# Half of a bias addition on VectorE, statistics in SBUF, and two tables made one stage later

## The chip, the cores and the metric

One core of a Trainium2 chip runs the whole program in one launch. The metric is device time in microseconds (us) of one execution; lower is better. The engines are TensorE (PE in the profile), VectorE (DVE), ScalarE (ACT), GpSimd (POOL) and SyncE (SP), whose queue issues most of the transfers.

## The reference

A graph network with four residual layers over 100,000 nodes of 128 features and 50,000 edges, sorted by their receiver. Each layer ends in a layer norm. The change touches the first one:

```python
h = x @ W                                   # 4 heads of 32 columns
alpha = leaky_relu(s_src[row] + s_dst[col])
...
alpha_n = ex / denom[row]
out = segment_sum(alpha_n * h[col], col) + bias
x = layernorm(x + out)
```

Since the weight of a message depends on its receiver's own row `h[col]`, the sum over the edges of one receiver is that row times a sum of weights for each head. So for a node that receives edges the kernel needs, per head, one total, and the layer becomes `layernorm(x + bias + totals * (x @ W))`.

## The kernel before

The program runs nine stages one after the other (`prepare`, `scores_and_sort`, `gat_softmax`, `gat_sums`, `first_layer`, `attention`, `gcn_first`, `gcn_second`, `final_edges`). Each stage ends in `end_stage`, a barrier of all engines. Within a stage every engine runs its own list of instructions, and the engines are ordered by semaphores alone: `then_inc` raises one when an instruction is done, `wait_ge` holds the engine's queue until it is reached.

`gat_sums` sums the attention weights over the edges of each receiver and leaves the totals, turned, in the table `K["totB"]` (128 x 6 x 392: four heads, the degree, and a position). VectorE and ScalarE copy it out of PSUM (L1304, L1337). Then ScalarE takes the root of the degree (L1339), and VectorE makes, in a chain of twenty instructions over 128 x 392 elements (L1308 to L1328), two index tables for later gathers (`idx_a`, `idx_b`) and five tables made from the degree (`dinvB`, `dlastB`, `dinv2B`, `dlast2B`, `degepsB`). In such a chain each instruction waits for the one before it (`link`).

`first_layer` handles the edges in 49 items of 1024 rows, 8 rows on each of 128 partitions. Tiles come in four buffers `u` (`x`, `y`, `o`, the norm's small tiles) or in two (`xT`, `hp`); `tp` has one. For each item:

- SyncE loads `x` (L1456). The load of an item waits until the add (below) of the item four before it is done. SyncE also stores the result `o` (L1460); in its queue the store of an item comes behind the load of the item six later.
- TensorE turns `x` into `tp` (L1483), ScalarE copies that to `xT` (L1499), TensorE multiplies by the weights into `hp` (L1490).
- GpSimd adds the bias to `x` in place (`shift`, L1469), once `x` is turned.
- VectorE multiplies `hp` by the totals of the heads into `y` (`scale`, L1508).
- GpSimd adds `x` to `y` (`add`, L1474).
- VectorE measures mean and variance (`norm_measure`, L1382 to L1399), ScalarE takes the root (L1408), VectorE forms `rs` and `nb` (`norm_scale`, L1419 and L1425), ScalarE applies them in eight instructions (`norm_apply`, L1433).

The order on each engine is written out by hand: `pipeline(engine, (part, lag, count), ...)` runs, in slot s, each part for item s - lag, in the order given:

```python
pipeline(sp, (load, 0, EIGHTS), (store, 6, EIGHTS))
pipeline(pool, (add, 3, EIGHTS), (shift, 1, EIGHTS))
pipeline(pe, (multiply, 1, EIGHTS), (turn, 0, EIGHTS))
pipeline(dve, (measure, 4, EIGHTS), (scale, 2, EIGHTS), (norm_scale, 4, EIGHTS))
```

(ScalarE: copy with lag 0, root with 4, apply with 5; the part names are shortened for `norm_scale`.)

Where the statistics lie is a choice of `norm_of`. Without `ps` all its small tiles are in SBUF. With `ps`, as `first_layer` calls it, the raw statistics, `gap`, `sums` and `squares` lie in one PSUM tile `small`; the odd half of the statistics is first copied to SBUF (L1388), and a second subtraction writes `gap` (L1391) beside `diff` (L1392).

Of the kernel before, what the change touches and what calls it, by code (L numbers as in the profile page):

```python
# [15 lines left out]
ALU = mybir.AluOpType  # L16
ACT = mybir.ActivationFunctionType
F32 = mybir.dt.float32
I32 = mybir.dt.int32

P = 128
N = 100000
E = 50000
D = 128
HEADS = 4
HC = D // HEADS
CHUNKS = 392
EP = CHUNKS * P
SORTN = 65536
SORTF = SORTN // P  # L30
G = 8
# [5 lines left out]
EIGHTS = CHUNKS // 8  # L37
# [1202 lines left out]
def gat_sums(nc, A, T, K):  # L1240
    with ExitStack() as ctx:
# [4 lines left out]
        quarter = CHUNKS // 4  # L1246
        rows = sb("rows", [P, HEADS + 2, 4 * P])
        roots = sb("roots", [P, CHUNKS])
        fallback, known, place = sb("fallback", [P, CHUNKS]), sb("known", [P, CHUNKS]), sb("place", [P, CHUNKS])
        where, bits = sb("where", [P, CHUNKS], I32), sb("bits", [P, CHUNKS], I32)  # L1250
        shift = sb("shift", [P, CHUNKS])
        turned = [ps(f"turned{i}", [P, 4, P]) for i in range(2)]
        turner = turner_of(sb, ps, sem)
        loaded, chain_v, raw_zero = sem("loaded"), sem("chain_v"), sem("raw_zero")
        totals_ready, totals_stored, rows_loaded = sem("totals_ready"), sem("totals_stored"), sem("rows_loaded")
        rows_turned, rows_taken, roots_ready, line_ready, line_stored = sem("rows_turned"), sem("rows_taken"), sem("roots_ready"), sem("line_ready"), sem("line_stored")
        rows_zero, taken_by_act = sem("rows_zero"), sem("taken_by_act")
        warm = sb("warm", [P, 1])
        block = ctx.enter_context(nc.Block())
# [30 lines left out]
        @block.vector  # L1290
        def _(dve):
            link = chain_of(dve, chain_v)
            dve.memset(raw[96:P, E % CHUNKS:, :], 0.0).then_inc(raw_zero, 1)
            link(dve.memset(turner["scr"][:], 0.0))
            link(dve.memset(v[:, HEADS, :], 1.0))
            dve.wait_ge(loaded, 64)
            link(dve.tensor_copy(v[:, 0:HEADS, :], raw[:, :, 0:HEADS].rearrange("p f h -> p h f")))
            link(dve.tensor_copy(v[:, HEADS + 1, :], raw[:, :, HEADS]))
            segment_scan(dve, link, turner, K["seg"], "sum", run[:], v[:, 0:HEADS + 1, :])
            segment_scan(dve, link, turner, K["seg"], "rise", v[:, 0:HEADS + 1, :], run[:])  # L1300
            dve.sem_inc(totals_ready, 1)
            for h in range(0, HEADS + 2, 2):
                dve.wait_ge(rows_turned, h + 1)
                dve.tensor_copy(K["totB"][:, h, :].rearrange("p (r b) -> p b r", b=4), turned[0][:, :, 0:quarter]).then_inc(rows_taken, 1)  # L1304
            dve.wait_ge(taken_by_act, HEADS // 2 + 1)
            dve.wait_ge(rows_taken, HEADS // 2 + 1)
            pos = K["totB"][:, HEADS + 1, :]
            link(dve.tensor_scalar(fallback[:], K["src_idx"][:, 0:CHUNKS], float(EP), None, ALU.add))  # L1308
            link(dve.tensor_scalar(known[:], pos, 0.0, None, ALU.is_ge))
            link(dve.tensor_copy(where[:], pos))  # L1310
            link(dve.tensor_scalar(bits[:], where[:], P - 1, None, ALU.bitwise_and))
            link(dve.tensor_scalar(where[:], where[:], 3 * P, None, ALU.bitwise_and))
            link(dve.tensor_copy(place[:], bits[:]))
            link(dve.tensor_copy(shift[:], where[:]))
            link(dve.scalar_tensor_tensor(out=place[:], in0=place[:], scalar=3.0, in1=pos, op0=ALU.mult, op1=ALU.add))
            link(dve.scalar_tensor_tensor(out=place[:], in0=shift[:], scalar=-127.0 / 128.0, in1=place[:], op0=ALU.mult, op1=ALU.add))
            link(dve.tensor_tensor(place[:], place[:], fallback[:], ALU.subtract))
            link(dve.tensor_tensor(place[:], place[:], known[:], ALU.mult))
            link(dve.tensor_tensor(place[:], place[:], fallback[:], ALU.add))
            link(dve.tensor_copy(K["idx_a"][:], place[:]))  # L1320
            link(dve.tensor_scalar(known[:], known[:], float(T12_Z), None, ALU.mult))
            link(dve.tensor_tensor(K["idx_b"][:], place[:], known[:], ALU.add))
            dve.wait_ge(roots_ready, 1)
            link(dve.reciprocal(K["dinvB"][:], K["dsqrtB"][:]))
            link(dve.tensor_tensor(K["dlastB"][:], K["dinvB"][:], K["lastB"][:], ALU.mult))
            link(dve.tensor_tensor(K["dinv2B"][:], K["dinvB"][:], K["dinvB"][:], ALU.mult))
            link(dve.tensor_tensor(K["dlast2B"][:], K["dinv2B"][:], K["lastB"][:], ALU.mult))
            link(dve.tensor_scalar(K["degepsB"][:], K["dinv2B"][:], EPS * D, None, ALU.mult))  # L1328

        @block.scalar  # L1330
        def _(act):
            act.activation(warm[:], K["one"][:], ACT.Sqrt)
            act.wait_ge(totals_ready, 1)
            act.activation(roots[:], v[:, HEADS, :], ACT.Sqrt, bias=K["one"][:, 0:1]).then_inc(line_ready, 1)
            for h in range(1, HEADS + 2, 2):
                act.wait_ge(rows_turned, h + 1)
                act.copy(K["totB"][:, h, :].rearrange("p (r b) -> p b r", b=4), turned[1][:, :, 0:quarter]).then_inc(taken_by_act, 1)  # L1337
            act.wait_ge(rows_taken, HEADS // 2 + 1)
            act.activation(K["dsqrtB"][:], K["totB"][:, HEADS, :], ACT.Sqrt, bias=K["one"][:, 0:1]).then_inc(roots_ready, 1)  # L1339

        @block.tensor
        def _(pe):
# [92 lines left out]
    ac.then_inc(norm["normed"][u], 1)  # L1435


def first_layer(nc, A, T, K):
    with ExitStack() as ctx:
        sb, ps, sem, sems, owned = stage_makers(nc, ctx, "l0")  # L1440
# [1 line left out]
        xT = [sb(f"xT{v}", [P, G, P]) for v in range(2)]  # L1442
        y = [sb(f"y{u}", [P, G, D]) for u in range(BUFS)]
        o = [sb(f"o{u}", [P, G, ROW1]) for u in range(BUFS)]
        tp = ps("tp", [P, G, P])
        hp = [ps(f"hp{v}", [P, G, D]) for v in range(2)]
        loaded, turned, copied, multiplied = sems("loaded"), sems("turned"), sems("copied"), sems("multiplied")
        shifted, scaled, summed, stored, o_set = sems("shifted"), sems("scaled"), sems("summed"), sems("stored"), sem("o_set")
        norm = norm_of(sb, sems, K["eps"], y, [tile[:, :, 0:D] for tile in o], width=G, ps=ps)
        block = ctx.enter_context(nc.Block())  # L1450

        @block.sync
        def _(sp):
            def load(t, u):
                wait_item(sp, summed, t, u, 4)
                sp.dma_start(as_tile_rows(x[u][:]), tile_rows(T["xdst"], t, u, G)).then_inc(loaded[u], 16)  # L1456

            def store(t, u):
                sp.wait_ge(norm["normed"][u], t + 1)
                sp.dma_start(tile_rows(T["t12"][0:EP], t, u, G), as_tile_rows(o[u][:])).then_inc(stored[u], 16)  # L1460
            pipeline(sp, (load, 0, EIGHTS), (store, 6, EIGHTS))
            for u in range(BUFS):
                sp.wait_ge(stored[u], 16 * per_buf(EIGHTS)[u])

        @block.gpsimd
        def _(pool):
            def shift(t, u):
                pool.wait_ge(turned[u], t + 1)
                pool.tensor_tensor(x[u][:], x[u][:], K["bias0"][:].unsqueeze(1).broadcast_to([P, G, D]), ALU.add).then_inc(shifted[u], 1)  # L1469

            def add(t, u):
                pool.wait_ge(shifted[u], t + 1)
                pool.wait_ge(scaled[u], t + 1)
                pool.tensor_tensor(y[u][:], y[u][:], x[u][:], ALU.add).then_inc(summed[u], 1)  # L1474
            pipeline(pool, (add, 3, EIGHTS), (shift, 1, EIGHTS))
# [26 lines left out]

        @block.vector
        def _(dve):
            def scale(t, u):
                dve.wait_ge(multiplied[u], t + 1)
                wait_item(dve, norm["normed"], t, u, 4)
                dve.tensor_tensor(y[u][:].rearrange("p j (a c) -> p j a c", a=HEADS),  # L1508
                                  hp[u % 2][:].rearrange("p j (a c) -> p j a c", a=HEADS),
                                  eight_each(K["totB"], t, u)[:, 0:HEADS].rearrange("p a j -> p j a").unsqueeze(3).broadcast_to([P, G, HEADS, HC]),  # L1510
                                  ALU.mult).then_inc(scaled[u], 1)

            def measure(t, u):
                dve.wait_ge(summed[u], t + 1)
                norm_measure(norm, dve, t, u)
            for u in range(BUFS):
                dve.memset(o[u][:, :, D:ROW1], 1.0).then_inc(o_set, 1)
            pipeline(dve, (measure, 4, EIGHTS), (scale, 2, EIGHTS), (lambda t, u: norm_scale(norm, dve, t, u), 4, EIGHTS))
    end_stage(nc, owned)


# [960 lines left out]
```

## Time and profile before

| | us |
|---|---|
| median of 3 runs | 5165.31 (5158.11 to 5167.69) |
| the profiled execution | 5164.06 |
| its span, first to last instruction | 5162.2 |
| `gat_sums` from its last table copy on: ScalarE's last start | 2200.22 |
| first load of `first_layer` issued | 2213.43 |
| first issue of `attention` | 2495.02 |

The profile is one execution on the chip. Starts are counted from the begin of the span. In a timeline each row gives the start, the busy time, engine, line, operation, `out<-in` by the tiles' names, the shape, and in brackets the idle time before it with what ended it. Tiles of `first_layer` are named `l_...` there (`l_small` is the PSUM tile of the statistics), those of `gat_sums` `gsu_...`, those of the stage `gat_softmax` `gsm_...`, of `scores_and_sort` `sort_...`, of `final_edges` `mss_...`; `kept_...` tiles live through the program and `t_...` are tables in HBM (`t_t` is the table that `first_layer` stores to).

### The profile page before, as it was taken

To read this page: it belongs to the slowest core of one execution; us is meant where nothing else is said; L and a number is where in the kernel's file an instruction comes from. 1 tells how busy PE (TensorE), PEld (TensorE's weight loads), DVE (VectorE), ACT (ScalarE), POOL (GpSimd) and SP (SyncE) were. 2 spreads that over 40 slices of the span, in tenths; PEclk is the share of its full clock that TensorE was granted. 3 is DMA by queue.
4 is the path that set the end of the run, shared out by engine and by line. 5 is a ranking of instruction groups with operands and counts; after the bars stand their busy time and mean duration, and the time that the engine had idled before them with its cause. 6 is when DMAs were issued, how large, how long until landed. Compare 5 with 4: busy or idle time off the path is not lost. (4 is left out here: it accounts for less than half of the span.)

```text
span 5162.2 us, 72321 instructions
## 1 busy us (share of the span) xinstructions
PE 3180.8 (62%) x15758; PEld 2424.3 (47%) x15758; DVE 3401.2 (66%) x11834; ACT 2870.2 (56%) x7165; POOL 3661.0 (71%) x3635
## 2 busy tenths in 40 slices
PE   3545555536662566256477746766888787777773
PEld 3545555534441444155466644444555465555552
DVE  6587555558887777467499973333677766566664
ACT  0105666638883888358357762333455566666663
POOL 5777777767775777468677717776777677777777
PEclk9555555559986988689689878888556599898987
DMA  2326777868882777446478858887677632222222
GB/s 72 78 71 207 238 240 238 241 129 250 251 250 63 223 228 224 128 149 202 137 200 223 220 158 249 224 226 206 192 210 208 182 77 73 71 73 70 71 73 60
DMA packets 821519, 862.51 MB, mean 167 GB/s; under 512 B 161544, under 2 KB 595309, under 8 KB 820667
## 3 DMA queue, kind: packets, MB, share of 16 engines
q1 hardware_dynamic: 705096, 673.45, 42.5%
q0 software_dynamic: 112896, 179.36, 15.6%
q10 hardware_dynamic: 3314, 7.36, 0.4%
q8 instruction: 72, 1.18, 0.1%
q14 instruction: 141, 1.16, 0.1%
HBM read 494.56 MB, written 370.75 MB: 168 GB/s over the span
## 5 line engine op out<-in xcount | busy, mean ns | idle before, releaser
L1929 POOL DMA_INDIRECT gs_xs<-t_t,kept_idx_b x392 | 369.8, 943 | 229.2 <-issue 118.9
L1035 POOL DMA_INDIRECT t_alpha<-gsm_raw,gsm_edge_idx x392 | 386.2, 985 | 165.8 <-issue 117.7
L2193 POOL DMA_INDIRECT mss_xs<-t_x,kept_idx_a x392 | 388.1, 990 | 144.8 <-issue 117.9
L2185 POOL DMA_INDIRECT out_dram<-mss_o,kept_scat_idx x392 | 395.5, 1009 | 119.4 <-issue 118.5
L534 POOL DMA_INDIRECT sort_xd<-in_x_dram,kept_dst_idx x392 | 380.1, 970 | 140.3 <-issue 118.5
L2049 POOL DMA_INDIRECT gs_xs<-t_z,kept_idx_a x392 | 379.2, 967 | 139.2 <-issue 119.2
L1598 POOL DMA_INDIRECT att_xs<-t_t,kept_idx_a x392 | 371.8, 948 | 134.2 <-issue 116.4
L1025 POOL DMA_INDIRECT gsm_raw<-t_al,kept_idx_b x392 | 378.8, 966 | 124.2 <-issue 118.9
L1227 PE MATMUL gsm_hp<-kept_w,gsm_zT 128*128 128x128 f32 x1568 | 257.8, 314 | 337.1 <-ACT gsm_zT L1093 337.1
L536 POOL DMA_INDIRECT sort_xs<-in_x_dram,kept_src_idx x392 | 379.4, 968 | 119.5 <-issue 118.6
L216 PE MATMUL gs_tp<-kept_ident,gs_xs 128*128 128x128 f32 x784 | 268.2, 361 | 267.8 <-DMA gs_xs<-t_t,kept_idx_b 146.1
L1227 PEld LDWEIGHTS gsm_hp<-kept_w,gsm_zT 128*128 128x128 f32 x1568 | 216.7, 214 | 388.3 <-ACT gsm_zT L1093 388.3
L755 PE MATMUL sort_tpd<-kept_ident,sort_xd 128*128 128x128 f32 x392 | 108.9, 434 | 384.3 <-DMA sort_xs<-in_x_dram,kept_src_idx 384.3
L1433 ACT ACTIVATE gsm_o<-gsm_y,gsm_nb,gsm_rs 128x128 f32<-128x128 f32 x784 | 323.7, 490 | 24.0 <-DVE gsm_nb L1425 23.4
L2006 DVE TENSOR_TENSOR_SCAN gs_sc<-gs_goes,gs_sc,gs_tp 128x512 f32<-128x512 uint8 x98 | 125.4, 1280 | 315.6 <-PE gs_tp L217 315.6
L793 ACT COPY sort_al<-sort_sps 128x16 f32<-128x16 f32 x98 | 16.8, 171 | 549.3 <-PE sort_sps L765 549.1
L216 PEld LDWEIGHTS gs_tp<-kept_ident,gs_xs 128*128 128x128 f32 x784 | 144.5, 184 | 371.4 <-DMA gs_xs<-t_t,kept_idx_b 178.2
L2311 ACT ACTIVATE mss_o<-mss_y,mss_nb,mss_rs 128x128 f32<-128x128 f32 x392 | 161.2, 482 | 280.3 <-DMA out_dram<-mss_o,kept_scat_idx 277.5
L1433 ACT ACTIVATE sort_o<-sort_x,sort_nb,sort_rs 128x128 f32<-128x128 f32 x792 | 312.2, 488 | 0.8 <-DMA t_t<-sort_o 0.8
L1991 ACT ACTIVATE gs_o<-gs_hp,kept_dlast2B 128x128 f32<-128x128 f32 x392 | 112.2, 369 | 312.1 <-PE gs_hp L1976 307.1
L217 PE MATMUL gs_tp<-kept_ident,gs_own 128*128 128x128 f32 x784 | 263.5, 354 | 0.0
L755 PEld LDWEIGHTS sort_tpd<-kept_ident,sort_xd 128*128 128x128 f32 x392 | 73.4, 225 | 391.7 <-DMA sort_xs<-in_x_dram,kept_src_idx 391.7
(556 smaller groups left out, 11061.9 us busy)
## 6 DMA issues: line engine op xcount, KB each, us to landing
t_t<-sort_o SPq DMA_DIRECT2D x66, 792.0 KB
t_x<-gsm_o SPq DMA_DIRECT2D x196, 264.0 KB
sort_x<-in_x_dram SPq DMA_DIRECT2D x66, 768.0 KB
gsm_x<-t_t SPq DMA_DIRECT2D x196, 256.0 KB
t_z<-gsm_z SPq DMA_DIRECT2D x196, 256.0 KB
out_dram<-gsm_o SPq DMA_DIRECT2D x196, 256.0 KB, 3.1
t_t<-l_o SPq DMA_DIRECT2D x49, 528.0 KB, 3.1
att_own<-t_t SPq DMA_DIRECT2D x98, 264.0 KB
```

The source lines that it names most:

```text
L216: pe.matmul(out, lhsT=a, rhs=ident[:], start=True, stop=False, is_transpose=True)
L534: pool.indirect_dma_start(xd[u][:, j, :], None, A["x"], bass.IndirectOffsetOnAxis(K["dst_idx"][:, c:c + 1], 0)).then_inc(gathered[u], 16)
L536: pool.indirect_dma_start(xs[u][:, j, :], None, A["x"], bass.IndirectOffsetOnAxis(K["src_idx"][:, c:c + 1], 0)).then_inc(gathered[u], 16)
L1025: pool.indirect_dma_start(raw[:, c, 0:HEADS], None, T["al"], bass.IndirectOffsetOnAxis(from_idx[:, c:c + 1], 0)).then_inc(gathered[u], 16)
L1035: pool.indirect_dma_start(T["alpha"], bass.IndirectOffsetOnAxis(edge_idx[:, c:c + 1], 0), raw[:, c, :], None).then_inc(scattered[u], 16)
L1227: mm = pe.matmul(hp[u % 2][:, j, :], zT[u][:, j, :], K["w1"][:], start=True, stop=True)
L1433: ac = act.activation(norm["o"][u][:, g, :], norm["y"][u][:, g, :], ACT.Identity, bias=norm["nb"][u][:, g:g + 1], scale=norm["rs"][u][:, g ...
L1598: pool.indirect_dma_start(xs[:, q % RING, j, :], None, T["t12"][0:EP + N], bass.IndirectOffsetOnAxis(K["idx_a"][:, c:c + 1], 0)).then_inc( ...
L1929: pool.indirect_dma_start(xs[u][:, j, :], None, T["t12"], bass.IndirectOffsetOnAxis(K["idx_b"][:, c:c + 1], 0)).then_inc(gathered[u], 16)
L2049: pool.indirect_dma_start(xs[u][:, j, :], None, T["z1"], bass.IndirectOffsetOnAxis(K["idx_a"][:, c:c + 1], 0)).then_inc(gathered[u], 16)
L2185: pool.indirect_dma_start(T["out"], bass.IndirectOffsetOnAxis(K["scat_idx"][:, c:c + 1], 0), o[q % BUFS][:, j, :], None, bounds_check=N - ...
L2193: pool.indirect_dma_start(xs[q % BUFS][:, j, :], None, T["x3"], bass.IndirectOffsetOnAxis(K["idx_a"][:, c:c + 1], 0)).then_inc(gathered[q ...
```

## The change

Three things change, all between the end of `gat_sums` and the end of `first_layer`:

1. The twenty-instruction chain leaves the end of VectorE's list in `gat_sums` and stands at the begin of VectorE's list in `first_layer`, behind four memsets and ahead of the loop. Its scratch tiles move with it. The semaphore between ScalarE's root and the chain goes, since the stages' barrier stands between them.
2. The bias is added to the first four of the eight rows of an item by GpSimd, and to the other four by VectorE, in a part with lag 1 that stands between `scale` and `norm_scale`. GpSimd's `add` waits for both.
3. `norm_of` is called without `ps`: the statistics lie in SBUF, and the copy of the odd half and the second subtraction go.

```diff
@@ gat_sums: VectorE
             dve.wait_ge(rows_taken, HEADS // 2 + 1)
-            pos = K["totB"][:, HEADS + 1, :]
-            link(dve.tensor_scalar(fallback[:], K["src_idx"][:, 0:CHUNKS], float(EP), None, ALU.add))
-            link(dve.tensor_scalar(known[:], pos, 0.0, None, ALU.is_ge))
...
-            link(dve.tensor_tensor(K["idx_b"][:], place[:], known[:], ALU.add))
-            dve.wait_ge(roots_ready, 1)
-            link(dve.reciprocal(K["dinvB"][:], K["dsqrtB"][:]))
-            link(dve.tensor_tensor(K["dlastB"][:], K["dinvB"][:], K["lastB"][:], ALU.mult))
-            link(dve.tensor_tensor(K["dinv2B"][:], K["dinvB"][:], K["dinvB"][:], ALU.mult))
-            link(dve.tensor_tensor(K["dlast2B"][:], K["dinv2B"][:], K["lastB"][:], ALU.mult))
-            link(dve.tensor_scalar(K["degepsB"][:], K["dinv2B"][:], EPS * D, None, ALU.mult))
@@ gat_sums: ScalarE
-            act.activation(K["dsqrtB"][:], K["totB"][:, HEADS, :], ACT.Sqrt, bias=K["one"][:, 0:1]).then_inc(roots_ready, 1)
+            act.activation(K["dsqrtB"][:], K["totB"][:, HEADS, :], ACT.Sqrt, bias=K["one"][:, 0:1])
+HALF = G // 2
@@ first_layer
+        chain_v = sem("chain_v")
+        other_shifted = sems("other_shifted")
-        norm = norm_of(sb, sems, K["eps"], y, [tile[:, :, 0:D] for tile in o], width=G, ps=ps)
+        norm = norm_of(sb, sems, K["eps"], y, [tile[:, :, 0:D] for tile in o], width=G)
@@ first_layer: GpSimd
                 pool.wait_ge(turned[u], t + 1)
-                pool.tensor_tensor(x[u][:], x[u][:], K["bias0"][:].unsqueeze(1).broadcast_to([P, G, D]), ALU.add).then_inc(shifted[u], 1)
+                pool.tensor_tensor(x[u][:, 0:HALF], x[u][:, 0:HALF], K["bias0"][:].unsqueeze(1).broadcast_to([P, HALF, D]), ALU.add).then_inc(shifted[u], 1)
             def add(t, u):
                 pool.wait_ge(shifted[u], t + 1)
+                pool.wait_ge(other_shifted[u], t + 1)
                 pool.wait_ge(scaled[u], t + 1)
@@ first_layer: VectorE
+            def shift(t, u):
+                dve.wait_ge(turned[u], t + 1)
+                dve.tensor_tensor(x[u][:, HALF:G], x[u][:, HALF:G], K["bias0"][:].unsqueeze(1).broadcast_to([P, G - HALF, D]), ALU.add).then_inc(other_shifted[u], 1)
             for u in range(BUFS):
                 dve.memset(o[u][:, :, D:ROW1], 1.0).then_inc(o_set, 1)
-            pipeline(dve, (measure, 4, EIGHTS), (scale, 2, EIGHTS), (lambda t, u: norm_scale(norm, dve, t, u), 4, EIGHTS))
+            link = chain_of(dve, chain_v)
+            pos = K["totB"][:, HEADS + 1, :]
+            link(dve.tensor_scalar(fallback[:], K["src_idx"][:, 0:CHUNKS], float(EP), None, ALU.add))
...
+            link(dve.tensor_scalar(K["degepsB"][:], K["dinv2B"][:], EPS * D, None, ALU.mult))
+            pipeline(dve, (measure, 4, EIGHTS), (scale, 2, EIGHTS), (shift, 1, EIGHTS), (lambda t, u: norm_scale(norm, dve, t, u), 4, EIGHTS))
```

## Rows read from the trace of the kernel before

**Rows 1.** The page's first line:
```profile
span 5162.2 us, 72321 instructions
```

**Rows 2.** Timeline of the joint of the two stages: start, busy us, engine, instruction:
```profile
2200.22 0.61 ACT L1339 ACTIVATE kept_dsqrtB<-kept_totB,kept_one 128x392 f32<-128x392 f32 x1
2200.46 0.36 DVE L1308 TENSOR_SCALAR gsu_fallback<-kept_src_idx 128x392 f32<-128x392 int32 x1 [0.66 <-ACT kept_totB L1337]
...
2212.09 0.36 DVE L1328 TENSOR_SCALAR kept_degepsB<-kept_dinv2B 128x392 f32<-128x392 f32 x1
2213.43 17.13 SPq L1456 DMA_DIRECT2D l_x<-t_xdst  x5
2213.53 0.21 DVE L1517 MEMSET l_o<- 128x32 f32 x4 [1.07 <-PEq L93]
...
2224.18 1.23 DVE L1508 TENSOR_TENSOR l_y<-l_hp,kept_totB 128x1024 f32<-128x1024 f32 x1 [10.45 <-PE l_hp L1490]
...
2227.82 2.35 POOL L1474 TENSOR_TENSOR l_y<-l_y,l_x 128x1024 f32<-128x1024 f32 x1
...
2228.62 1.23 DVE L1508 TENSOR_TENSOR l_y<-l_hp,kept_totB 128x1024 f32<-128x1024 f32 x1 [3.21 <-PE l_hp L1490]
```

**Rows 3.** Busy time by stretch: length, PE, PEld, DVE, ACT, POOL (instructions), granted clock, DMA:
```profile
2252.30:2468.50 216.20, 138.57 (x984) 122.30 (x984) 166.77 (x738) 175.60 (x410) 190.87 (x83) 0.94 0.62 200
```

**Rows 4.** Timeline inside that stretch:
```profile
2336.58 1.01 ACT L1499 COPY l_xT<-l_tp 128x1024 f32<-128x1024 f32 x1 [0.55 <-PE l_tp L1483]
...
2341.06 0.39 SPq L1460 DMA_DIRECT2D t_t<-l_o  x1
...
2341.65 0.38 SPq L1456 DMA_DIRECT2D l_x<-t_xdst  x1
...
2345.96 1.09 PE L1483 MATMUL l_tp<-kept_ident,l_x 128*128 128x128 f32 x8 [0.78 <-DMA l_x<-t_xdst]
...
2347.09 1.01 ACT L1499 COPY l_xT<-l_tp 128x1024 f32<-128x1024 f32 x1 [0.74 <-PE l_tp L1483]
```

**Rows 5.** Waits in that stretch: total us, times, longest:
```profile
PE l_tp L1483 <- DMA l_x<-t_xdst: 29.6, 31, 1.7
```

**Rows 6.** Timeline of VectorE from one item's statistics to the next:
```profile
2239.11 1.64 DVE L1382 BATCH_NORM_STATS2 l_small<-l_y 128x6 f32<-128x128 f32 x8
...
2241.72 1.22 DVE L1508 TENSOR_TENSOR l_y<-l_hp,kept_totB 128x1024 f32<-128x1024 f32 x1
...
2242.85 0.19 DVE L1419 RECIPROCAL l_rs<-l_sd 128x8 f32<-128x8 f32 x1
...
2243.08 0.17 DVE L1425 SCALAR_TENSOR_TENSOR l_nb<-l_small,l_rs 128x8 f32<-128x8 f32 x1
```

**Rows 7.** Timeline of VectorE in `gat_softmax`, whose statistics lie in SBUF:
```profile
2006.08 0.87 DVE L1382 BATCH_NORM_STATS2 gsm_stats<-gsm_y 128x6 f32<-128x128 f32 x4
...
2007.56 0.16 DVE L1399 TENSOR_TENSOR gsm_mv<-gsm_mv,gsm_diff 128x4 f32<-128x4 f32 x1
```

**Rows 8.** Single lines: shortest/median/longest in ns, first and last start:
```profile
L658 DVE TENSOR_TENSOR sort_moved<-sort_merged x16: 691/692/693, 379.4 to 424.5; 128x512 f32<-128x512 f32 x16
L1474 POOL TENSOR_TENSOR l_y<-l_y,l_x x49: 2334/2354/2379, 2227.8 to 2478.3; 128x1024 f32<-128x1024 f32 x49
L2338 DVE TENSOR_TENSOR mss_tmp<-mss_tmp x98: 291/292/358, 4156.1 to 5087.7; 128x128 f32<-128x128 f32 x98
```

**Rows 9.** Timeline in `scores_and_sort`, VectorE beside GpSimd's gathers:
```profile
431.31 0.69 DVE L730 TENSOR_TENSOR sort_moved<-sort_moved,sort_swaps 128x512 f32<-128x512 f32 x1
431.47 1.35 POOL L534 DMA_INDIRECT sort_xd<-in_x_dram,kept_dst_idx  x1 [0.30 <-issue]
...
433.10 1.75 DVE L736 TENSOR_TENSOR sort_x<-sort_x,sort_shift 128x1536 f32<-128x1536 f32 x1
433.12 0.94 POOL L536 DMA_INDIRECT sort_xs<-in_x_dram,kept_src_idx  x1 [0.30 <-issue]
```

**Rows 10.** Timeline: the last scaling of `first_layer`:
```profile
2476.97 1.22 DVE L1508 TENSOR_TENSOR l_y<-l_hp,kept_totB 128x1024 f32<-128x1024 f32 x1
```

More of the change, by code:

```diff
@@ L1248, in gat_sums @@
         roots = sb("roots", [P, CHUNKS])
-        fallback, known, place = sb("fallback", [P, CHUNKS]), sb("known", [P, CHUNKS]), sb("place", [P, CHUNKS])
-        where, bits = sb("where", [P, CHUNKS], I32), sb("bits", [P, CHUNKS], I32)
-        shift = sb("shift", [P, CHUNKS])
         turned = [ps(f"turned{i}", [P, 4, P]) for i in range(2)]
@@ L1255, in gat_sums @@
         totals_ready, totals_stored, rows_loaded = sem("totals_ready"), sem("totals_stored"), sem("rows_loaded")
-        rows_turned, rows_taken, roots_ready, line_ready, line_stored = sem("rows_turned"), sem("rows_taken"), sem("roots_ready"), sem("line_ready"), sem("line_stored")
+        rows_turned, rows_taken, line_ready, line_stored = sem("rows_turned"), sem("rows_taken"), sem("line_ready"), sem("line_stored")
         rows_zero, taken_by_act = sem("rows_zero"), sem("taken_by_act")
@@ L1306, in _ @@
             dve.wait_ge(rows_taken, HEADS // 2 + 1)
-            pos = K["totB"][:, HEADS + 1, :]
-            link(dve.tensor_scalar(fallback[:], K["src_idx"][:, 0:CHUNKS], float(EP), None, ALU.add))
-            link(dve.tensor_scalar(known[:], pos, 0.0, None, ALU.is_ge))
[L1310 to L1321, printed above, removed]
-            link(dve.tensor_tensor(K["idx_b"][:], place[:], known[:], ALU.add))
-            dve.wait_ge(roots_ready, 1)
-            link(dve.reciprocal(K["dinvB"][:], K["dsqrtB"][:]))
-            link(dve.tensor_tensor(K["dlastB"][:], K["dinvB"][:], K["lastB"][:], ALU.mult))
-            link(dve.tensor_tensor(K["dinv2B"][:], K["dinvB"][:], K["dinvB"][:], ALU.mult))
-            link(dve.tensor_tensor(K["dlast2B"][:], K["dinv2B"][:], K["lastB"][:], ALU.mult))
-            link(dve.tensor_scalar(K["degepsB"][:], K["dinv2B"][:], EPS * D, None, ALU.mult))
         @block.scalar
@@ L1444, in first_layer @@
         o = [sb(f"o{u}", [P, G, ROW1]) for u in range(BUFS)]
+        fallback, known, place = sb("fallback", [P, CHUNKS]), sb("known", [P, CHUNKS]), sb("place", [P, CHUNKS])
+        where, bits = sb("where", [P, CHUNKS], I32), sb("bits", [P, CHUNKS], I32)
+        shift_of = sb("shift_of", [P, CHUNKS])
+        chain_v = sem("chain_v")
         tp = ps("tp", [P, G, P])
@@ L1517, in _ @@
                 dve.memset(o[u][:, :, D:ROW1], 1.0).then_inc(o_set, 1)
-            pipeline(dve, (measure, 4, EIGHTS), (scale, 2, EIGHTS), (lambda t, u: norm_scale(norm, dve, t, u), 4, EIGHTS))
+            link = chain_of(dve, chain_v)
+            pos = K["totB"][:, HEADS + 1, :]
+            link(dve.tensor_scalar(fallback[:], K["src_idx"][:, 0:CHUNKS], float(EP), None, ALU.add))
+            link(dve.tensor_scalar(known[:], pos, 0.0, None, ALU.is_ge))
+            link(dve.tensor_copy(where[:], pos))
+            link(dve.tensor_scalar(bits[:], where[:], P - 1, None, ALU.bitwise_and))
+            link(dve.tensor_scalar(where[:], where[:], 3 * P, None, ALU.bitwise_and))
+            link(dve.tensor_copy(place[:], bits[:]))
+            link(dve.tensor_copy(shift_of[:], where[:]))
+            link(dve.scalar_tensor_tensor(out=place[:], in0=place[:], scalar=3.0, in1=pos, op0=ALU.mult, op1=ALU.add))
+            link(dve.scalar_tensor_tensor(out=place[:], in0=shift_of[:], scalar=-127.0 / 128.0, in1=place[:], op0=ALU.mult, op1=ALU.add))
+            link(dve.tensor_tensor(place[:], place[:], fallback[:], ALU.subtract))
+            link(dve.tensor_tensor(place[:], place[:], known[:], ALU.mult))
+            link(dve.tensor_tensor(place[:], place[:], fallback[:], ALU.add))
+            link(dve.tensor_copy(K["idx_a"][:], place[:]))
+            link(dve.tensor_scalar(known[:], known[:], float(T12_Z), None, ALU.mult))
+            link(dve.tensor_tensor(K["idx_b"][:], place[:], known[:], ALU.add))
+            link(dve.reciprocal(K["dinvB"][:], K["dsqrtB"][:]))
+            link(dve.tensor_tensor(K["dlastB"][:], K["dinvB"][:], K["lastB"][:], ALU.mult))
+            link(dve.tensor_tensor(K["dinv2B"][:], K["dinvB"][:], K["dinvB"][:], ALU.mult))
+            link(dve.tensor_tensor(K["dlast2B"][:], K["dinv2B"][:], K["lastB"][:], ALU.mult))
+            link(dve.tensor_scalar(K["degepsB"][:], K["dinv2B"][:], EPS * D, None, ALU.mult))
+            pipeline(dve, (measure, 4, EIGHTS), (scale, 2, EIGHTS), (shift, 1, EIGHTS), (lambda t, u: norm_scale(norm, dve, t, u), 4, EIGHTS))
     end_stage(nc, owned)
```

## Prediction

> **What bounds the kernel now.** I read the page first: the span is 5162.2 us [rows 1], and the profiled execution as a whole took 5164.06 us, 1.9 us around the span. The change touches the joint between two stages and the whole of `first_layer`, so the timeline of the joint came next [rows 2]. ScalarE's last work in `gat_sums` is the root, over at 2200.22 + 0.61 = 2200.83 us. VectorE then works alone on the tables until 2212.09 + 0.36 = 2212.45 us, and the first load of the next stage is issued 0.98 us later. So 11.62 us of the span are nothing but table making.
>
> Then the loop of `first_layer`, by the busy times of its even stretch [rows 3]: ScalarE runs 10 instructions an item (copy, root, eight normalizations), so its 410 in 216.20 us are 41 items, at 5.27 us each. GpSimd is busiest there (190.87 us), but it is not what sets the rate; the timeline shows a loop over two items [rows 4]. A copy begins at 2336.58, ScalarE then normalizes, the store goes out at 2341.06 and SyncE's next load, queued behind it, at 2341.65; the data let TensorE start at 2345.96, and the copy after that begins at 2347.09: 10.51 us for two items. The chain of waits agrees: TensorE's transposes waited 29.6 us for that load [rows 5]. VectorE and GpSimd only follow.
>
> **The tables.** All twenty instructions go from the end of `gat_sums` to the begin of `first_layer` on VectorE; SyncE, TensorE and ScalarE start their stage 11.62 us earlier. The chain lasts 2212.45 - 2200.46 = 11.99 us; from 2213.53 - 11.62 + 0.21 (memsets) = 2202.1 it runs to 2214.1, then come the new half shift of item 0 (0.69, below) and its scaling (1.23) until 2216.1. GpSimd's first add, for which that scaling is needed, began at 2227.82 us [rows 2], which is 2216.2 us after the same shift: GpSimd was still adding the bias of item 1. So the cover is there and the head start of 11.6 us survives up to the first add. Were VectorE not covered it would cost the 2.3 us by which the scaling is late (2216.1 against 2224.18 + 1.23 - 11.62 = 2213.8). The chain issues no transfer and passes none; its index tables are next read by gathers behind the stage's barrier, its degree tables later still. The root's semaphore goes; GpSimd's add gets one wait more, for VectorE's half shift, which lies a slot or more ahead of it.
>
> **VectorE's slot, unhindered.** Start to start: scaling to reciprocal 2242.85 - 2241.72 = 1.13 (the next instruction starts 0.09 before the former ends), reciprocal to `nb` 0.23, `nb` (0.17 long) to statistics 0.08, statistics to scaling 2241.72 - 2239.11 = 2.61 [rows 6]; together 4.05 us. With the statistics in SBUF the copy of the odd part and one subtraction go: another stage that has this form takes 2007.56 - (2006.08 + 0.87) = 0.61 us from the end of its sums to the last addition [rows 7], and an addition over 128x512 takes 0.692 us [rows 8]. So the new slot is 1.13 + 0.61 (shift, next start 0.08 before its end) + 0.23 + 0.08 + (1.64 + 0.61 + 0.17 - 0.09 = 2.33) = 4.38 us, 0.89 below 5.27. GpSimd drops from 2 x 2.35 [rows 8] to about 2.35 + 1.2 an item. If nothing else happened, neither engine would be felt: a better balance that moves no bound, and the load loop keeps 5.27 us.
>
> **The price that does not stand in the plan.** Today every VectorE instruction of this loop that takes two tensors has one of them in PSUM. After the change seven an item (the shift, three on the statistics' halves, square, sum, `nb`) have both in SBUF. Rows elsewhere show what that does beside GpSimd [rows 9]. A VectorE addition from SBUF and SBUF began at 431.31 (0.69 long); GpSimd's gather issued at 431.47 lasted 1.35 us instead of 0.94: longer by 0.41, where 0.53 of the VectorE instruction were left, so GpSimd got on 0.12 before it ended. Beside the addition at 433.10, 1.75 us long but with `sort_shift` in PSUM, the gather lasted its 0.94. So one waits for the other, and only when VectorE reads two SBUF tensors. The reverse is there, small: line 2338 (both inputs SBUF) has a longest of 358 ns against a median of 292 [rows 8]. A gather reads one column of indices; the adds of GpSimd read two tensors of 1024 all through their 2.35 us, and beside today's VectorE they never vary: 2334 to 2379 ns. How long VectorE stands behind such an add no row shows. Bounds: 0.07 us (the 358 against 292) and the rest of the add, up to 2.35. I take the upper one, because the add reads SBUF until it ends.
>
> The Trainium skill, "SBUF — State Buffer", section "Who interferes with whom", speaks against this change in the same direction: a VectorE instruction with two SBUF inputs contends with a GpSimd instruction that reads SBUF, and whichever comes second is blocked for the whole of the first. The gather's row agrees for VectorE first; for a long GpSimd instruction first, no row shows it. By this rule the wait is the upper bound, by the rows alone anything between the two.
>
> **The slot with that wait.** Time 0 is the start of the shift. The scaling ends at 0.09 and releases GpSimd's add, which must stand behind the shift until 0.69 - 0.12 = 0.57 and ends at 0.57 + 2.35 = 2.92. `nb` is ready at 0.61 + 0.23 = 0.84 and waits until 2.92: 2.08 us. GpSimd's half shift goes next, behind `nb`, from about 3.1 to 4.3, and the statistics (one input each) run from 3.00 to 4.64, so the steps behind them find GpSimd idle. Slot: 4.38 + 2.08 = 6.46 us, and VectorE becomes the bound; behind its late scaling wait GpSimd's add, with it SyncE's load, and TensorE's multiply two items on. ScalarE's copy, root and normalizing fit, as they fit in 5.27 today.
>
> **The sum.** Start: the scaling of item 1 ends at about 2228.62 + 1.23 - 11.62 = 2218.2 [rows 2]; the shift behind it waits for add 0 (from 2216.6 to 2219.0), the statistics' steps of item 0 for add 1 (to 2223.0) and perhaps a half shift of 1.2; the scaling of item 2 ends at 2224.9 to 2226.1, taken as 2225.5. From it to the scaling of item 48 are 46 slots: 2225.5 + 46 x 6.46 = 2522.7, against 2476.97 + 1.22 = 2478.2 now [rows 10]: 44.5 us later. In the tail one `nb` more waits, +2.1, and two measurements are 0.28 shorter, -0.6. Total +46 us, the saved 11.6 already in it: 5164.1 + 46 = 5210 for the profiled time, 5211 for the median, which lies 1.25 higher. Later stages follow the barrier unchanged.
>
> **The rivals.**
> *VectorE is hardly held up.* If a long GpSimd add lets VectorE in between its reads (the 0.07 us of line 2338 seven times, 0.5 us), the slot stays under 5.27, the load loop rules, and what is left is the head start: 5165.3 - 11.6 = 5154 us, faster. For it speaks that only short waits of VectorE are on record; against it, that GpSimd's gather waited out a VectorE instruction to within 0.12 us. It decides where 2225.5 + 46 T equals 2478.2, at T = 5.49, a wait of 1.1 us a slot.
> *GpSimd keeps SBUF for its next instruction too.* Its instructions follow each other with no gap; if `nb` stands behind the half shift as well, the slot is 6.46 + 1.2 = 7.66: 2225.5 + 46 x 7.66 = 2577.9, +99.7 + 1.5 = +101, 5266 us.
> *In between:* VectorE is slowed, not stopped, about 1 us a slot; T near 5.4, and the loss eats the head start: 5150 to 5190 us.
>
> **How the numbers follow.** VectorE behind one add 0.55 (5195 to 5230 with a slot of 6.1 to 6.9), behind both 0.20, in between 0.10, hardly held up 0.15. The likeliest gives 5211. The range 5185 to 5275 holds the first two and the upper part of the third. A measurement of this kernel tells about 0.2%, 10 us, from no change. Slower: 0.55 + 0.20 + 0.04 = 0.79. The rival without a wait lies at -11.6, barely past 10, so its 0.15 are split 0.09 faster and 0.06 same; with the rest of the in-between, 0.11 same and 0.10 faster.
>
> **What would show it.** Right: the load of item 0 at about 2201.8; the tables right behind the memsets; copies about 6.5 us apart; `nb`, 0.17 us now, lasting or idling some 2 us; GpSimd's add longer by 0.3 to 0.5 us behind the shift; transposes no longer waiting for the load. Wrong: `nb` and the shift at their 0.17 and 0.69 us with copies 5.27 apart (first rival), or `nb` beginning only after the half shift (second). A stage that begins less than 11 us earlier would make the head's term wrong.

## The result, and the profile of the changed kernel

The changed kernel takes 5204.5 us (median of 4 runs, 5201.9 to 5207.7) against 5165.8 before (4 runs, 5158.1 to 5167.7): 38.7 us more, a ratio of 1.0076 with a 95% interval of 1.0063 to 1.0088. The prediction was 5211, within 5185 to 5275.

The page's first line, to be held against [rows 1]:

```profile
span 5204.1 us, 72263 instructions
```

The timeline of the joint, the counterpart of [rows 2] (start, length, engine, instruction, idle time before it and what ended it):

```profile
2199.71 0.61 ACT L1314 ACTIVATE kept_dsqrtB<-kept_totB,kept_one 128x392 f32<-128x392 f32 x1
2201.04 28.77 SPq L1439 DMA_DIRECT2D l_x<-t_xdst  x7
...
2201.26 0.33 DVE L1508 TENSOR_SCALAR l_fallback<-kept_src_idx 128x392 f32<-128x392 int32 x1
...
2206.87 1.26 POOL L1452 TENSOR_TENSOR l_x<-l_x,kept_bias 128x512 f32<-128x512 f32 x1 [57.03 <-PE l_tp L1467]
...
2207.01 1.34 DVE L1520 CAST kept_idx_a<-l_place 128x392 int32<-128x392 f32 x1
...
2212.89 1.43 POOL L1452 TENSOR_TENSOR l_x<-l_x,kept_bias 128x512 f32<-128x512 f32 x1 [4.75 <-PE l_tp L1467]
2213.23 1.52 DVE L1526 TENSOR_TENSOR kept_dlast2B<-kept_dinv2B,kept_lastB 128x392 f32<-128x392 f32 x1
...
2214.78 0.36 DVE L1527 TENSOR_SCALAR kept_degepsB<-kept_dinv2B 128x392 f32<-128x392 f32 x1
...
2215.79 1.22 DVE L1496 TENSOR_TENSOR l_y<-l_hp,kept_totB 128x1024 f32<-128x1024 f32 x1
...
2217.18 2.63 POOL L1458 TENSOR_TENSOR l_y<-l_y,l_x 128x1024 f32<-128x1024 f32 x1 [2.86 <-DVE l_y L1496]
```

The first load goes out 12.39 us earlier than at 2213.43. The root before it also began 0.51 us earlier in this execution, which is no work of the change, so the head start is 11.9 us. GpSimd's first addition of items began at 2227.82 and begins at 2217.18 now, 10.64 us earlier. The head start was there; the loop behind it spent it.

The loop's busy time by stretch, in the columns of [rows 3], the counterpart of that row:

```profile
2252.30:2508.50 256.20, 167.29 (x962) 156.90 (x961) 249.88 (x681) 171.46 (x400) 154.94 (x81) 0.77 0.51 165
```

ScalarE's 400 instructions are 40 items in 256.20 us, 6.41 us an item instead of 5.27. VectorE is busy for 249.88 of them (98%), where it was busy for 166.77 of 216.20 before: it is the bound now. But it was given only some 0.33 us an item more to do (the prediction's slots of 4.38 and 4.05 us), so most of its new busy time is not work. The timeline of one item's slot shows what it is (VectorE's part answers to [rows 6]):

```profile
2333.70 1.23 DVE L1496 TENSOR_TENSOR l_y<-l_hp,kept_totB 128x1024 f32<-128x1024 f32 x1
...
2334.84 0.68 DVE L1491 TENSOR_TENSOR l_x<-l_x,kept_bias 128x512 f32<-128x512 f32 x1
...
2335.09 2.65 POOL L1458 TENSOR_TENSOR l_y<-l_y,l_x 128x1024 f32<-128x1024 f32 x1 [2.54 <-DVE l_y L1496]
2335.44 0.20 DVE L1394 RECIPROCAL l_rs<-l_sd 128x8 f32<-128x8 f32 x1
2335.67 2.10 DVE L1400 SCALAR_TENSOR_TENSOR l_nb<-l_mv,l_rs 128x8 f32<-128x8 f32 x1
...
2337.69 1.63 DVE L1357 BATCH_NORM_STATS2 l_stats<-l_y 128x6 f32<-128x128 f32 x8
2337.70 1.27 POOL L1452 TENSOR_TENSOR l_x<-l_x,kept_bias 128x512 f32<-128x512 f32 x1
...
2339.36 0.17 DVE L1367 TENSOR_TENSOR l_diff<-l_stats 128x8 f32<-128x8 f32 x1
...
2340.12 1.23 DVE L1496 TENSOR_TENSOR l_y<-l_hp,kept_totB 128x1024 f32<-128x1024 f32 x1
```

`nb` works on 8 numbers a partition and lasts 2.10 us: it begins 0.58 us into GpSimd's addition and ends 0.03 us behind that addition's end. This is how such a stall looks here. It is not an idle time with a releaser in brackets, so the list of waits does not have it; it is a tiny instruction with a long duration, and the busy share counts it as work. The statistics behind it have one input and run at their usual 1.63 us beside GpSimd's half shift.

TensorE's granted clock is lower in this stretch too, 0.77 instead of 0.94, but that is not what costs the time: the multiplies of one item (L1474) take between 2.02 and 3.76 us from slot to slot, while 36 slots in a row from 2269.52 on (scaling to scaling) last 6.40 to 6.44 us whatever the multiplies take.

Over all items, the lines of the three instructions in question (shortest, median and longest in ns, first and last start). The second answers to GpSimd's row in [rows 8]:

```profile
L1400 DVE SCALAR_TENSOR_TENSOR l_nb<-l_mv,l_rs x49: 166/2094/2102, 2227.4 to 2527.7; 128x8 f32<-128x8 f32 x49
L1458 POOL TENSOR_TENSOR l_y<-l_y,l_x x49: 2342/2645/2653, 2217.2 to 2520.8; 128x1024 f32<-128x1024 f32 x49
L1491 DVE TENSOR_TENSOR l_x<-l_x,kept_bias x49: 679/681/1709, 2215.2 to 2514.3; 128x512 f32<-128x512 f32 x49
```

GpSimd's addition is itself 0.29 us longer at the median (2354 before): it begins while VectorE's half shift still runs and stands until that is nearly through. Behind the scalings, which now come late, the others wait. The head of the list of waits from 2252 to 2500 (total us, times, longest) no longer has the transposes' wait for the load of [rows 5]. Two of its rows name VectorE's scaling; in the third ScalarE's copy waits for transposes that stand behind the multiply of the second row in TensorE's list:

```profile
POOL l_y L1458 <- DVE l_y L1496: 98.7, 39, 2.6
PE l_hp L1474 <- DVE l_y L1496: 83.1, 34, 3.5
ACT l_xT L1483 <- PE l_tp L1467: 73.1, 34, 3.5
```

The last scaling, against [rows 10], and the first issue of the stage behind the barrier, which stood at 2495.02 before:

```profile
2519.45 1.22 DVE L1496 TENSOR_TENSOR l_y<-l_hp,kept_totB 128x1024 f32<-128x1024 f32 x1
...
2537.59 2.74 SPq L1616 DMA_DIRECT2D att_xd<-t_t  x4
```

That stage starts 42.6 us later, and the two profiled spans differ by 41.9, so the loss is made ahead of it.

### The profile page after: what moved, and what is told of

Same layout as the page of the kernel before. It is cut to its first block and busy times, and to the rows that moved or that the text cites. A ratio compares the mean times of both kernels' runs of the same rounds, so it can differ in the third digit from the quotient of the medians.

```text
span 5204.1 us, 72263 instructions
## 1 busy us (share of the span) xinstructions
PE 3224.3 (62%) x15758; PEld 2478.6 (48%) x15758; DVE 3506.4 (67%) x11785; ACT 2870.0 (55%) x7165; POOL 3620.6 (70%) x3635
```

## The experiments

The leading theory, "the port": a VectorE instruction that reads two tensors from SBUF can't run beside a GpSimd instruction that does so too; the second stands until the first ends. The rivals were that VectorE simply has too much work since the change ("VectorE's load"), and that GpSimd, once it has SBUF, keeps it for its next instruction as well. The first four runs take the change apart.

**The tables alone.** The changed kernel with the statistics in PSUM and the whole bias on GpSimd, as before:

```diff
-        norm = norm_of(..., width=G)
+        norm = norm_of(..., width=G, ps=ps)
-                pool.tensor_tensor(x[u][:, 0:HALF], ...).then_inc(shifted[u], 1)
+                pool.tensor_tensor(x[u][:], ...).then_inc(shifted[u], 1)
...
-                pool.wait_ge(other_shifted[u], t + 1)
...
-                dve.tensor_tensor(x[u][:, HALF:G], ...).then_inc(other_shifted[u], 1)
```

> Only the tables move; bias whole on GpSimd, statistics in PSUM. Port theory: the head start of 11.6 us, less some 2 us, because the chain's casts and two-input steps now stand behind GpSimd's whole bias additions of items 0 and 1 (2.35 us each): 5154 to 5157 us. Rival, VectorE's load: nothing is added to an item, so the full 11.6 us: 5154. A loss in the head as large as the gain (5165) would speak against both.

Measured: 5155.2 us (5152.0 to 5162.1) against 5165.7, ratio 0.9981 (0.9972 to 0.9990): 10.4 us less. The move of the tables is a gain by itself, and the 11.6 us of head start lie inside its interval (some 5 to 14 us). The timeline of its joint shows two table steps that stood behind GpSimd's bias additions; whether the time felt them, the medians cannot tell:

```profile
2205.83 2.38 POOL L1451 TENSOR_TENSOR l_x<-l_x,kept_bias 128x1024 f32<-128x1024 f32 x1 [57.24 <-PE l_tp L1465]
...
2206.04 2.39 DVE L1514 CAST kept_idx_a<-l_place 128x392 int32<-128x392 f32 x1
...
2212.03 2.35 POOL L1451 TENSOR_TENSOR l_x<-l_x,kept_bias 128x1024 f32<-128x1024 f32 x1 [3.82 <-PE l_tp L1465]
2212.11 2.69 DVE L1518 TENSOR_TENSOR kept_dlastB<-kept_dinvB,kept_lastB 128x392 f32<-128x392 f32 x1
```

The cast and the product stand until the addition beside them is over. In the kernel before, where GpSimd is idle, the same two take 0.36 and 0.57 us:

```profile
2206.26 0.36 DVE L1320 CAST kept_idx_a<-gsu_place 128x392 int32<-128x392 f32 x1
...
2210.29 0.57 DVE L1325 TENSOR_TENSOR kept_dlastB<-kept_dinvB,kept_lastB 128x392 f32<-128x392 f32 x1
```

**Half of the bias on VectorE alone.** The kernel before, with this:

```diff
-                pool.tensor_tensor(x[u][:], ...).then_inc(shifted[u], 1)
+                pool.tensor_tensor(x[u][:, 0:HALF], ...).then_inc(shifted[u], 1)
...
+                pool.wait_ge(other_shifted[u], t + 1)
...
+                dve.tensor_tensor(x[u][:, HALF:G], ...).then_inc(other_shifted[u], 1)
```

> Only half of the bias goes to VectorE. Port theory: the half addition starts while GpSimd is idle, nothing with two SBUF inputs stands behind GpSimd's add, the slot of 4.66 us hides under 5.27: 5160 to 5170 us, copies 5.2 to 5.3 us apart, GpSimd's add longer by about 0.3 us. Rival, VectorE's load (the added 0.6 us an item is what costs): most of the loss appears here, about 5200.

Measured: 5166.3 us (5163.8 to 5174.6), ratio 1.0003 (0.9993 to 1.0012): no difference. GpSimd's additions were 2644 ns long at the median here too (2354 before), so the shift's own conflict is there, and it does not show in the rate: the scalings lie 5.31 us apart in the mean, as in the kernel before. That the load loop of [rows 4] covers it fits, but is not shown by this run. `nb`, with its sums in PSUM, kept its 166 ns.

**Statistics in SBUF alone.** The kernel before, with one line changed:

```diff
-        norm = norm_of(sb, sems, K["eps"], y, [...], width=G, ps=ps)
+        norm = norm_of(sb, sems, K["eps"], y, [...], width=G)
```

> Only the statistics go to SBUF; VectorE has less work an item (3.77 us unhindered against 4.05). Port theory: nb or the first subtraction stands behind the add, a later step behind the whole bias addition; slot 6.6 to 6.75 us, 5225 to 5235 us. Rival, VectorE's load: not slower, 5160 to 5166 us, copies 5.27 us apart.

Measured: 5224.6 us (5224.0 to 5224.7), ratio 1.0113 (1.0098 to 1.0129): 58.9 us more, although this edit takes two instructions an item away from VectorE and gives it none. It is 0.4 us below the range that the port theory gave. VectorE's load as a cause falls with this run. The timeline of one slot (scalings 6.57 us apart):

```profile
2335.07 0.17 DVE L1425 SCALAR_TENSOR_TENSOR l_nb<-l_mv,l_rs 128x8 f32<-128x8 f32 x1
2335.07 2.40 POOL L1474 TENSOR_TENSOR l_y<-l_y,l_x 128x1024 f32<-128x1024 f32 x1 [1.82 <-DVE l_y L1508]
...
2337.22 0.28 DVE L1392 TENSOR_TENSOR l_diff<-l_stats 128x8 f32<-128x8 f32 x1
...
2337.42 0.16 DVE L1393 TENSOR_TENSOR l_mv<-l_stats 128x8 f32<-128x8 f32 x1
2337.43 2.37 POOL L1469 TENSOR_TENSOR l_x<-l_x,kept_bias 128x1024 f32<-128x1024 f32 x1
2337.50 2.32 DVE L1394 TENSOR_TENSOR l_mv<-l_stats 128x8 f32<-128x8 f32 x1
```

Without a half shift on VectorE, `nb` begins with GpSimd's addition and goes through in 0.17 us. Of the two ways that were expected it is mostly the second: another instruction is the victim (`nb`'s median is 167 ns). The third step on the statistics stands behind the bias addition for 2.15 us (its median over the 49 items is 2324 ns). The two steps before it got in when the addition of items ended at 2337.47; the first of them waits for that end as well, by some 0.5 us at the median (669 ns). In other slots `nb` is caught, for up to 2036 ns. Which instruction is caught changes with the phase of the two engines; that one is caught stays.

**Tables and half shift, statistics in PSUM.** The changed kernel with one line put back:

```diff
-        norm = norm_of(..., width=G)
+        norm = norm_of(..., width=G, ps=ps)
```

> The change without its third part: statistics back in PSUM. Port theory: the slot is 4.66 us and hides, the head start of 11.6 us stays: 5152 to 5156 us, faster than before by 0.2%. Rival, VectorE's load: 4.66 us is more than the changed kernel's unhindered 4.38, so as slow or slower than the changed kernel: 5204 or more.

Measured: 5154.3 us (5151.8 to 5157.9), ratio 0.9979 (0.9970 to 0.9988). From here, placing the statistics in SBUF costs 5204.5 - 5154.3 = 50.2 us by the medians. And it cannot be told from the tables alone (5155.2): the half shift is worth nothing that shows in either setting.

**`nb` alone freed.** In the changed kernel only the sums go to PSUM, which of the later steps `nb` alone reads:

```diff
+        total = ps("total", [P, BUFS, G])
+        norm["sums"] = [total[:, u, :] for u in range(BUFS)]
```

> The changed kernel with one tile moved: the sums of the means lie in PSUM, so that nb alone no longer reads two SBUF tensors; the statistics stay in SBUF. Port theory: nb goes at once (0.17 us instead of 2.09), the statistics end before GpSimd's add does, and now the first subtraction waits some 0.3 us and the third some 1.2 us behind the half shift: slot 5.6 to 5.9 us, 5172 to 5185 us. Rival, VectorE's load: same work, so 5204. If the 2.09 us were nb's own and not a wait, 5204 too.

Measured: 5177.0 us (5174.2 to 5180.6) against 5166.7, ratio 1.0021 (1.0012 to 1.0030). Of the 50 us, 27.5 are given back by one operand's place. `nb` is at 166 ns for all 49 items, and the next two-input step is caught, behind the half shift (timeline):

```profile
2331.61 0.17 DVE L1400 SCALAR_TENSOR_TENSOR l_nb<-l_total,l_rs 128x8 f32<-128x8 f32 x1
...
2333.36 0.35 DVE L1367 TENSOR_TENSOR l_diff<-l_stats 128x8 f32<-128x8 f32 x1
...
2333.64 1.29 POOL L1454 TENSOR_TENSOR l_x<-l_x,kept_bias 128x512 f32<-128x512 f32 x1
2333.72 1.24 DVE L1369 TENSOR_TENSOR l_mv<-l_stats 128x8 f32<-128x8 f32 x1
```

**Hand-over.** In the changed kernel GpSimd makes the addition in two instructions, the second right behind the first:

```diff
-                pool.tensor_tensor(y[u][:], y[u][:], x[u][:], ALU.add).then_inc(summed[u], 1)
+                pool.tensor_tensor(y[u][:, 0:HALF], y[u][:, 0:HALF], x[u][:, 0:HALF], ALU.add)
+                pool.tensor_tensor(y[u][:, HALF:G], ..., ALU.add).then_inc(summed[u], 1)
```

> The changed kernel with GpSimd's add made in two instructions of four rows each. Port theory with a hand-over at each GpSimd instruction's end: nb waits for the first half only (about 0.95 us), the first subtraction for the end of the half shift (0.7): slot about 6.0 us instead of 6.4, 5183 to 5192 us. If GpSimd kept the port through instructions that follow each other, nb would stand behind three of them: slot 7.5 us or more, 5255 or more. If it let VectorE in between its reads, no change: 5204.

Measured: 5186.0 us (5185.5 to 5191.6), ratio 1.0039 (1.0025 to 1.0053). With the same work `nb` waits for one half only (median 1004 ns instead of 2094), and the slot falls to 6.03 us (timeline):

```profile
2335.29 1.56 POOL L1458 TENSOR_TENSOR l_y<-l_y,l_x 128x512 f32<-128x512 f32 x1 [2.01 <-DVE l_y L1497]
...
2335.86 1.00 DVE L1400 SCALAR_TENSOR_TENSOR l_nb<-l_mv,l_rs 128x8 f32<-128x8 f32 x1
...
2336.81 1.26 POOL L1459 TENSOR_TENSOR l_y<-l_y,l_x 128x512 f32<-128x512 f32 x1
...
2338.04 1.27 POOL L1452 TENSOR_TENSOR l_x<-l_x,kept_bias 128x512 f32<-128x512 f32 x1
...
2338.45 0.88 DVE L1367 TENSOR_TENSOR l_diff<-l_stats 128x8 f32<-128x8 f32 x1
```

`nb` ends with the first half, though the second is queued at once: SBUF changes hands at the end of each instruction here, and GpSimd does not keep it.

**The load loop opened.** [Rows 4] say that the kernel before waits for a load that is queued behind a store. Two runs let the store come one item later, so that the next load goes out ahead of it. First on tables with half shift (5154.3):

```diff
-            pipeline(sp, (load, 0, EIGHTS), (store, 6, EIGHTS))
+            pipeline(sp, (load, 0, EIGHTS), (store, 7, EIGHTS))
```

> Tables moved, half shift on VectorE, statistics in PSUM, and each store queued one load later (lag 7 instead of 6). If the loop over two items through store and load sets the 5.27 us, as the prediction read it, it opens: the next to bind are VectorE (4.66), ScalarE (4.5) and the add-load-turn path (about 4.7): 4.7 to 4.8 us an item, 5127 to 5135 us. If something else sets the rate: 5154.

Measured: 5143.0 us (5141.4 to 5145.3), ratio 0.9952 (0.9939 to 0.9966). The loop was a bound, for the time falls by 11.2 us; but it falls less than expected, a miss of 8 us. Its busy times by stretch, and two multiplies of TensorE with the scalings of VectorE that come behind each:

```profile
2260.00:2440.00 180.00, 121.03 (x840) 112.24 (x840) 163.10 (x670) 149.01 (x351) 136.57 (x71) 0.90 0.65 207
```

```profile
2292.76 2.02 PE L1474 MATMUL l_hp<-kept_wh,l_xT 128*128 128x128 f32 x16 [1.88 <-DVE l_y L1496]
...
2296.15 1.22 DVE L1496 TENSOR_TENSOR l_y<-l_hp,kept_totB 128x1024 f32<-128x1024 f32 x1
...
2301.32 1.22 DVE L1496 TENSOR_TENSOR l_y<-l_hp,kept_totB 128x1024 f32<-128x1024 f32 x1
...
2302.70 3.57 PE L1474 MATMUL l_hp<-kept_wh,l_xT 128*128 128x128 f32 x16 [2.10 <-DVE l_y L1496]
...
2306.08 1.22 DVE L1496 TENSOR_TENSOR l_y<-l_hp,kept_totB 128x1024 f32<-128x1024 f32 x1
...
2311.75 1.23 DVE L1496 TENSOR_TENSOR l_y<-l_hp,kept_totB 128x1024 f32<-128x1024 f32 x1 [0.24 <-ACT l_o L1408]
```

The 35 items there take 5.1 us each, and no engine is full over the whole stretch. TensorE waits for VectorE's scaling ahead of many multiplies; about 11 of 38 then last 3.3 to 3.65 us instead of 2.02, and the granted clock in the stretch of the second line shown (2302.60 to 2306.30) is 0.54, near the lower of its two levels, 1.2 GHz, while it is 1.00 in that of the first. The timeline shows what they cost: the 11 slots of VectorE (scaling to scaling, from 2260 to 2450) that come behind one of these slow multiplies last 5.57 to 5.86 us (5.71 in the mean; here 2311.75 - 2306.08 = 5.67), the 26 others 4.66 to 5.21 us (4.84; most of them 4.76, the scaling at 2306.08 after that at 2301.32). By this, an estimate, the slow multiplies cost 11 x 0.87 / 37 = 0.26 us a slot, some 12 us in 46 slots, which is more than the miss. Why the one multiply is granted less than the other stays open, since TensorE's idle time just ahead of the two hardly differs (2.10 and 1.88 us); and that the slow multiplies cause the miss is read from the trace alone: no run separates it.

Second, the same lag with the tables alone, the whole bias on GpSimd:

```diff
-            pipeline(sp, (load, 0, EIGHTS), (store, 6, EIGHTS))
+            pipeline(sp, (load, 0, EIGHTS), (store, 7, EIGHTS))
```

> The same with the bias whole on GpSimd: GpSimd needs 2 x 2.31 = 4.62 us an item and its add can start only behind the whole addition. If GpSimd is then the bound, 4.7 to 4.9 us an item: 5130 to 5142 us, slower than with the half shift; if the half shift is worth nothing, as fast as that. If the store-load loop does not set the rate: 5155.

Measured: 5132.2 us (5127.7 to 5133.1), ratio 0.9927 (0.9914 to 0.9941), faster than both kernels and than the run before it. The same view of it:

```profile
2260.00:2440.00 180.00, 119.10 (x905) 105.48 (x904) 155.59 (x689) 164.39 (x386) 177.54 (x77) 0.98 0.71 224
```

38.6 items at 4.66 us, with GpSimd busy for 177.54 of 180 us: its two additions of some 2.35 us an item are the bound. One might expect the half shift to help once GpSimd is full; but the run with it, which has GpSimd at 136.57 us, is 11 us slower.

## Why the prediction was right

**The tables' head start** (forecast 11.62 us): 11.9 were measured, the root's earlier start taken off.

**The chain and the start of the loop:** here the working missed something small. The chain was to end at 2214.1 and ended at 2215.14, although the execution was 0.51 us early: the cast of `idx_a` and one product lost about 1 us each behind GpSimd's half shifts. The prediction had named these conflicts for the loop, and had costed the chain as if GpSimd were idle. The scaling of item 2 ended at 2225.40 + 1.22 = 2226.62, forecast 2225.5.

**VectorE behind one addition** (wait 2.08 us, slot 6.46): the wait was 2.094 - 0.166 = 1.93 us and the slot (2520.67 - 2226.62) / 46 = 6.39. The wait is smaller because `nb` began 0.83 us behind the shift, as forecast, while GpSimd's addition ended at 2.90; the working then added 0.17 us of run time that the blocked instruction no longer needs, since it ends 0.03 us behind the addition. So the statistics begin 2.85 us behind the shift (forecast 3.00), and 0.10 us is lost again in the steps after them. Those steps found GpSimd idle, as forecast: its half shift ends at 2338.97, the first step begins at 2339.36. The addition was longer by 0.29 us (forecast 0.3 to 0.5).

**The sum.** The last scaling ended at 2520.67 instead of 2522.7. With the 0.51 us of the early execution put back that is 1.5 us short: 1.6 late at the start, 46 x 0.07 = 3.1 gained in the slots. Of the +1.5 expected in the tail 0.1 came (16.92 us from the last scaling to the next stage's first issue, 16.83 before): the `nb` that was to wait there began at 2520.81, 0.03 us ahead of GpSimd's addition, and took 0.17 us. So +43.1 at the barrier against +46, and 38.7 by the medians; the rest lies within the spread of single runs, some 5 us either way.

**The rivals.** "Hardly held up" would need waits under 1.1 us; there were 1.93 an item. "GpSimd keeps SBUF for its next instruction" fell with the split addition, and at the same place in the changed kernel: the statistics begin as the addition ends. "In between" fell too: for 46 of the 49 items `nb` lasts over 2 us and ends 0.01 to 0.04 us behind the addition (the other three, at the end of the loop, ran free at 0.17 us). Nor had the longer steps got on while they stood: the cast and the product of the tables-alone run, 0.36 and 0.57 us long when free, end 0.22 and 0.42 us behind GpSimd's addition. So they are stopped and not slowed.

The rule of the Trainium skill that the prediction weighed ("SBUF — State Buffer", section "Who interferes with whom") gave the upper bound, a block for the whole of the first instruction. The traces now agree for a long GpSimd instruction first: `nb` 2.10 us instead of 0.17, and 1.00 behind half an addition.

## What to carry to other kernels

Count, for each VectorE instruction that runs beside GpSimd, how many of the tensors it reads lie in SBUF: moving the small statistics from PSUM to SBUF removed two instructions an item and cost 50 us, because one 0.17 us instruction an item then waited out most of an addition of 2.6 us. Freeing that one instruction gave back only about half, since its neighbours were caught next. Look for it where a small instruction lasts long and ends with GpSimd's, not among the waits. And measure the parts of a bundled change one by one: this one held a gain of 10.4 us, a part worth nothing and a loss of 50, and the gain grew (to 34.5 us) when the bound of the loop, a load queued behind a store, was taken away with it.

## What was not expected of the hardware

A cast from f32 to int32 reads one tensor, and still stood behind GpSimd: 1.34 us beside a half shift, 2.39 beside a whole one, against 0.36 in the kernel before, where GpSimd was idle. Reciprocals of 128x8 (0.20 us) and the statistics (1.63 us) ran through beside such an addition. The Trainium skill's page "SBUF — State Buffer", in the same section, lists casts among the instructions that can contend; the two rows agree.

GpSimd can also get in between VectorE instructions that follow each other closely. Of three steps in a row on the statistics' halves, with the statistics in SBUF alone, two ran in 0.28 and 0.16 us and the third took 2.32, since the bias addition had begun 0.07 us before it.
